# Reordering SyncE's DMA issues and two VectorE steps in one iteration of a gated cross-attention kernel

## The reference, cut to what matters

```python
n = layernorm(x)
q, k, v = n @ Wq + bq, ctx @ Wk + bk, ctx @ Wv + bv      # 16 heads of 16
e = einsum('nqhd,nkhd->nhqk', q, k);  e = where(mask == 0, min, e)
a = einsum('nhqk,nkhd->nqhd', softmax(e / sqrt(16)), v)
x = x + tanh(g_xattn) * (a @ Wo + bo)
x = x + tanh(g_ffn) * tanh(layernorm(x) @ W1 @ W2 @ W3 + b_ffn)
```

## Time and profile before

| | |
|---|---|
| median of 3 runs | 1143.55 us (1141.15 to 1146.37) |
| the profiled execution, its own time | 1153.29 us |
| its span, first to last instruction | 1151.5 us |
| mean granted TensorE clock | 0.978 |
| PE busy | 1041.1 us, 90% |
| DVE, ACT, POOL busy | 937.6 us (81%), 834.5 us (72%), 801.2 us (70%) |
| DMA moved | 158.87 MB, mean 138 GB/s; SP's queue 48.5% of 16 engines |

### The profile page before, as it was taken

How to read it: one execution, slowest core, us unless ns; L and a number is a source line. 1 busy time by engine, 2 the same in 40 slices (tenths; PEclk the granted TensorE clock), 3 DMA queues, 4 the chain that set the end, 5 groups by cost and what they waited for, 6 DMA issues and landing times.

```text
span 1151.5 us, 45278 instructions
## 1 busy us (share of the span) xinstructions
PE 1041.1 (90%) x18487; PEld 905.1 (79%) x18487; DVE 937.6 (81%) x1331; ACT 834.5 (72%) x1275; POOL 801.2 (70%) x1184
## 2 busy tenths in 40 slices
PE   5989989999999999999999989989999999999964
PEld 4767878887888888888778778878788788888854
DVE  4778788788888888888888788788887787888766
ACT  4466778677787777777787777777776786777742
POOL 5256677677777777777777777677776676777753
PEclk9899999999999999999999999999998999999998
DMA  5134455555555555555555455555545454554432
GB/s 154 41 95 128 130 141 152 139 142 153 145 155 139 154 152 145 148 154 155 139 154 143 140 150 144 144 145 144 161 133 138 139 144 137 140 159 122 115 114 90
DMA packets 260400, 158.87 MB, mean 138 GB/s; under 512 B 174945, under 2 KB 227170, under 8 KB 260194
## 3 DMA queue, kind: packets, MB, share of 16 engines
q1 hardware_dynamic: 260050, 155.72, 48.5%
q10 hardware_dynamic: 144, 0.26, 0.1%
HBM read 85.92 MB, written 68.94 MB: 134 GB/s over the span
## 4 chain that ended last, share of the span: by engine, by line
PE 34%; DMA 26%; SPq 23%; issue 11%; DVE 5%; POOL 1%; ACT 0%; DVEq 0%; POOLq 0%
DMA scratch_y<-yn 12%; PE ps_m L502 8%; PE ps_s L623 6%; SPq L299 6%; PE ps_s L602 6%; DMA q_aug<-scratch_m 5%; SPq L288 4%; DMA scratch_m<-max_T 4%; PE ps_m L564 4%; PE ps_m L495 4%; SPq L271 3%; PE ps_x L634 2%; PE ps_s L608 2%; SPq L258 2%; SPq L281 2%
## 5 line engine op out<-in xcount | busy, mean ns | idle before, releaser
L1006 DVE TENSOR_TENSOR probs<-ps_s,far_T 128x2048 f32<-128x2048 f32 x128 | 293.3, 2291 | 99.5 <-PE ps_s L623 93.2
L995 DVE TENSOR_REDUCE neg_max<-ps_s 128x16 f32<-128x2048 f32 x128 | 292.6, 2286 | 60.0 <-PE ps_s L608 59.8
L797 ACT ACTIVATE probs<-probs 128x2048 f32<-128x2048 f32 x128 | 244.6, 1911 | 6.7 <-DVE probs L1006 6.6
L623 PE MATMUL ps_s<-q_aug,k_aug 32*128 32x128 f32 x4096 | 155.4, 289 | 62.7 <-DMA q_aug<-scratch_m 59.1
L623 PEld LDWEIGHTS ps_s<-q_aug,k_aug 32*128 32x128 f32 x4096 | 130.3, 191 | 83.4 <-DMA q_aug<-scratch_m 69.1
L413 POOL TENSOR_TENSOR cT<-ctx_T,cT 128x512 fp32r<-128x512 f32 x62 | 79.2, 1277 | 151.6 <-ACT cT L747 151.6
L772 ACT ACTIVATE q_aug<-ps_m,q_bias,q_scale 128x256 f32<-128x256 f32 x256 | 123.4, 562 | 70.9 <-PE ps_m L495 63.3
L602 PE MATMUL ps_s<-k_aug,q_aug 32*128 32x128 f32 x4096 | 151.9, 284 | 14.4 <-DVE probs L1006 7.4
L602 PEld LDWEIGHTS ps_s<-k_aug,q_aug 32*128 32x128 f32 x4096 | 129.3, 187 | 35.1 <-issue 27.4
L634 PE MATMUL ps_x<-probs,v_ones 128*32 128x128 f32 x4096 | 139.2, 277 | 3.2 <-issue 2.4
L772 ACT ACTIVATE k_aug<-ps_m,k_bias,parity 128x256 f32<-128x256 f32 x256 | 123.5, 564 | 18.1 <-PE ps_m L495 18.1
(11 more groups left out here) (123 smaller groups left out, 1789.5 us busy)
## 6 DMA issues: line engine op xcount, KB each, us to landing
scratch_a<-a_den SPq DMA_DIRECT2D x64, 512.0 KB, 3.4
x_in<-in_x SPq DMA_DIRECT2D x64, 256.0 KB, 3.9
a_rows<-scratch_a SPq DMA_DIRECT2D x64, 256.0 KB
den_wide<-scratch_r SPq DMA_DIRECT2D x64, 256.0 KB
out<-y SPq DMA_DIRECT2D x64, 256.0 KB, 4.9
ctx_in<-in_ctx SPq DMA_DIRECT2D x252, 64.0 KB, 3.4
scratch_y<-yn SPq DMA_DIRECT2D x59, 256.0 KB, 4.7
y_blocks<-scratch_y SPq DMA_DIRECT2D x236, 64.0 KB, 2.1
```

The lines of the kernel that those rows point to most:

```text
L623: last = nc.tensor.matmul(ps_s[:, j, s, :], k_aug[p % 2][rows, n, s, :], q_aug[p % 2][rows, n, s, :], start=True, stop=True, tile_position ...
L797: nc.scalar.activation(tile, tile, ACT.Exp).then_inc(probs_ready, 1)
L995: nc.vector.tensor_reduce(neg_max[:, 0:H].rearrange("p (j c) -> p j c", j=G), ps_s[:], AX.X, ALU.max, negate=True).then_inc(max_ready, 1)
L1006: nc.vector.tensor_tensor(probs[i % 2][:].rearrange("p j s q -> p (j s) q"), ps_s[:].rearrange("p j s q -> p (j s) q"), far_T[:].unsqueeze ...
```

## The change

In SP's loop:

- `load_ctx(t+3)` moves from behind `store` to behind `load_x`;
- `read_max(2t)` moves ahead of `write_a(t-2)` and `load_x(t+4)`, so that only `read_den` stands between it and `write_max(2t)`;
- `write_y(t-4)` moves from the end of the iteration to ahead of `read_max(2t+1)`, and so ahead of `read_wide(t-2)` too.

In DVE's loop `turn_max(2t)` moves ahead of `add_residual` and `turn_ctx`, `turn_ctx` goes behind `add_residual`, and `turn_max(2t+1)` moves ahead of `reciprocals`. Nothing is added or removed.

```diff
@@ SP
                 if is_pair(t - 7):
                     store(t - 7)
-                if is_pair(t + 3):
-                    load_ctx(t + 3)
                 if is_pair(t - 5):
                     read_y(t - 5)
                 write_max(2 * t)
                 if is_pair(t - 2):
                     read_den(t - 2)
+                read_max(2 * t)
+                if is_pair(t - 2):
                     write_a(t - 2)
                 if is_pair(t + 4):
                     load_x(t + 4)
-                read_max(2 * t)
+                if is_pair(t + 3):
+                    load_ctx(t + 3)
                 write_max(2 * t + 1)
                 if is_pair(t - 2):
                     write_reciprocals(t - 2)
                     read_a(t - 2)
+                if is_pair(t - 4) and t - 4 <= END:
+                    write_y(t - 4)
                 read_max(2 * t + 1)
                 if is_pair(t - 2):
                     read_wide(t - 2)
-                if is_pair(t - 4) and t - 4 <= END:
-                    write_y(t - 4)
@@ DVE
                     maxima(2 * t)
-                if is_pair(t + 2):
-                    turn_ctx(t + 2)
                 turn_max(2 * t)
                 if is_pair(t - 4):
                     add_residual(t - 4)
+                if is_pair(t + 2):
+                    turn_ctx(t + 2)
@@ DVE
                     maxima(2 * t + 1)
+                turn_max(2 * t + 1)
                 if is_pair(t - 2):
                     reciprocals(t - 2)
-                turn_max(2 * t + 1)
```

## The result

| | before | after |
|---|---|---|
| median, 9 runs each | 1143.04 us (1136.36 to 1151.53) | 1148.67 us (1141.73 to 1150.54) |
| ratio after to before | | 1.0069, 95% interval 1.0037 to 1.0102 |
| the profiled execution | 1153.29 us | 1147.69 us |
| its span, mean granted clock | 1151.5 us, 0.978 | 1145.9 us, 0.990 |
| median in a later comparison, on another chip | 1157.74 us | 1148.28 us, ratio 0.9939 (0.9910 to 0.9967) |

The forecast was 1131 us, a gain of 1.1%. In the comparison that answers to it the change costs 0.7%; in a later one it wins 0.6%. The changed kernel's time hardly moves between the two, that of the kernel before moves by 15 us. Why is part of what follows.

What follows compares the result with a forecast made beforehand. PE works 90% of the span; at most 59 us of its waits for late maxima could be won. A POOL ring of 16.8 against 17.02 us left 12.5 us: 1143.55 - 12.5 = 1131 us, range 1102 to 1163.

Steps and rivals of the forecast that it cites:

- The maxima: PE's wait ahead of scores_T(2t): even maxima come up to 2.3 us earlier, 59 us to be had.
- the ring: Loop from read_wide through POOL's divide_a to yn, then SP's write_y and back to read_wide: 16.8 us, the period's floor.
- The moved transfers: SP's load_ctx, write_a and load_x ahead of the odd write_max: 0.5 to 1.5 us later, covered, cost nothing.
- The new wait and its ring: SP's write_y waits for yn ahead of read_wide, closing a loop through POOL: 10.80 + 1.70 + L.
- L: Time from issue of read_wide to the start of the divide_a it releases: taken as 4.3 us, bounds 4.22 and 5.50.
- The frame: Time scale of one undisturbed PE iteration, scores(2t) at 608.29, the next at 624.27; old write_y put at 15.9 us.
- The first rival: The ring is slower than the old loop, L 4.8 to 5.09: 1160 to 1176 us, chance 0.23.
- The sum: Whole loop: 17.02 - 16.8 = 0.22 us in 57 iterations, 12.5 us off the median 1143.55, giving 1131 us.
- SP's own chain: Rival: SP's steps from write_y on, 16.85 us, set the period; loop at 17.0, 1140 to 1146 us, chance 0.2.
- Ring order: DMA queue rule: transfers behind read_wide never slowed it, write_y ahead does; L would stay about where it was.

Runs made afterwards that it cites:

- max_only: The kernel before with only read_max(2t) moved ahead of write_a and load_x: 1121.21 us, ratio 0.968.
- write_y_only: The kernel before with only write_y moved ahead of read_max(2t+1) and read_wide: 1151.17 us, ratio 0.995.
- ctx_first: The changed kernel with load_ctx alone put back behind store: 1151.68 us, ratio 0.995 to the kernel before.
- dve_only: The kernel before with only the DVE swaps (turn_max and turn_ctx order): 1151.07 us, ratio 0.998.
- wide_first: The changed kernel with read_wide moved ahead of write_y in SP's order: 1184.59 us, ratio 1.028 to the kernel before.
- ring_shorter: The changed kernel with POOL's add_out_bias moved from between divide_a and yn to behind yn: 1100.50 us, ratio 0.953 to the kernel before.
- ring_longer: The changed kernel with one extra 128 x 512 POOL step between divide_a and yn: 1191.54 us, ratio 1.034 to the kernel before.

## Why the prediction was wrong

**The maxima.** Right in the total: 59.1 us of waits fell to 1.6, and the mean granted clock went from 0.978 to 0.990. Not right in the parts. The prediction gave 1.8 of the 2.3 us to the earlier `write_y` and 0.5 to `read_max(2t)`. Alone, the move of `read_max` took these waits to 6.2 us (max_only) and the earlier `write_y` to 53.3 (write_y_only). The part that closes the ring was not the part that won the maxima.

**The moved transfers.** Right in the cost, nothing. The delay was overrated: in the rows above, the odd `write_max` is issued at 622.65, 1.2 us after its maxima are turned (621.20 + 0.21, DVE's timeline), inside the 0.5 to 1.5 us foreseen. But that is one of the later ones. In 30 of the 56 iterations it leaves within 0.1 us, and the mean is 0.34 us. No wait of PE for it appeared, and ctx_first shows that `load_ctx` costs nothing where it now stands, as long as the ring sets the pace.

**The new wait and its ring.** Right in the mechanism, and shown by dose and response. POOL's chain was put at 10.80 us (10.75 measured), SP's part at 1.70 (1.65), the release of PE by xn as described (62.8 us of waits). The 10.80 hold two shifts that cancel: on average xn is 0.4 us shorter and the short steps ahead of it 0.4 us longer than in the kernel before (the last section). The frame's 15.9 us for the old `write_y` should be 16.4 (624.66 - 608.29); nothing was worked out from it.

**L, the failed size.** I took 4.3 us "near the low end, because a write of y leaves SBUF quickly". No row showed a write of y ahead of that read, and L measured 4.57 on average. That makes the ring 16.99 instead of 16.8 us, which is 57 x 0.19 = 11 us. The forecast missed by 17.7. The first rival had its turning point at 4.52, and this is where the kernel landed, only far closer to it than the 4.8 to 5.09 that I had priced.

**The base of the difference, the failed step.** The sum took 17.02 us as the old period, from an execution of 1153.3 us, set the ring of 16.8 against it, and then carried the difference of 12.5 us over to the median of 1143.55. That is allowed only if both kernels scale alike. A ring made of POOL steps and one landing does not shrink when the other kernel has a good run. At the median of 1143.04 the old period is 17.02 - (1151.5 - 1141.2) / 57 = 16.84 us, with 1141.2 the median less the 1.8 us that lie around the span. Against it my own ring of 16.8 promised 2 us, "no change", and the measured 16.99 gives 57 x 0.15 = 8.6 us more, where 5.6 were measured between the medians. This step cost the forecast 57 x 0.18 = 10 us, about as much as L did. Comparing the ring with the old kernel's median, not with its profiled execution, would have given no change as the forecast, and "slower" a larger chance.

**Outside the loop, a term put at nothing.** "The first iterations have no y, and the tail is untouched" was not so. `turn_max` of iteration 6 starts at 121.00 us instead of 126.20, and from iteration 62 to the end of the span it is 73.6 us instead of 72.4, so 4.0 us were won outside the 56 iterations. The second profiles say the same (120.54 against 126.08, and 73.8 against 72.3). Which part of the change brings the start forward stays open (dve_only alone starts that step at 123.36). With it the account closes: 11 + 10 - 4 = 17 of the 17.7 us missed, and 8.6 - 4.0 = 4.6 of the 5.6 us between the medians.

**SP's own chain.** Its 16.85 us was too long: in the changed kernel SP waits 96.4 us for yn in 59 iterations, so its chain takes 17.0 - 1.6 = 15.4 us, and 0.4 us of that is waiting for max_T (21.8 us in the 56 iterations). The write of y lands in 3.2 us (median) and not in 4.7, since the 256 KB of `read_wide` are no longer just ahead of it (wide_first, which puts them back, has 4.9), and issuing ctx took 2.5 us in the median, not the 3.65 of the earlier trace rows, which was one of the slow ones in the kernel before as well (median 2.8).

**Ring order.** The Trainium skill (DMA: Bandwidth & Descriptors, Queues, rings and completion order) says that each DMA engine consumes descriptors in ring order. From that I had worked out that L would stay near 5.1. What stands behind `read_wide` indeed hardly matters: with ctx behind it L is 4.68 in ctx_first, without 4.57. But a write of y 1.6 us ahead slows it less than `read_a` 2 us ahead did (5.17 on average in the first profile of the kernel before, 4.89 in the second). The rule does not tell these two apart, and the measured 4.57 decides. How far ahead `read_a` stands goes with L: within ring_shorter L is 5.25 on average in the 15 iterations where it is 2.2 to 2.7 us ahead, and 4.64 in the 15 where it is 3.2 us or more.

## What to carry to other kernels

When a step that waits for another engine is moved ahead of others in a queue, follow what stands behind it until the path comes back to the same wait: if it does, the sum of that ring is a floor for the period, and idle time on the engines in it is no cover. Then compare the floor with the old kernel's own range of times, not with the one execution that was profiled, since waits that vary are replaced by one that does not. And once a ring is named, look for a step in it that nobody inside needs: here moving one 1.2 us addition out of it turned a change worth about nothing into one of 4.7%.

## What the runs showed of the hardware

A short step of POOL takes longer while a certain step of DVE runs. In the rows of the changed kernel above, a step on 128 x 4 elements at 621.48 takes 0.76 us, where its neighbours take 0.20. DVE's timeline has, at that time,

```profile
621.56 0.63 DVE L958 TENSOR_TENSOR yT<-y_T,yT 128x512 fp32r<-128x512 f32 x1
```

and the end of the POOL step (622.24) is just behind the end of this one (622.19). In the changed kernel 63 of these short steps (without L371, which takes 1.04 us in nearly every case) take over 0.4 us, and 58 of them overlap this DVE step; another 20 overlap it and stay short. One iteration earlier it is another step, again beside L958:

```profile
604.90 0.56 POOL L379 TENSOR_TENSOR ln_t<-ln_t 128x4 f32<-128x4 f32 x1
```

```profile
604.78 0.63 DVE L958 TENSOR_TENSOR yT<-y_T,yT 128x512 fp32r<-128x512 f32 x1
```

It belongs to the ring's 10.75 us. In the kernel before the same DVE step falls on xn: in the earlier trace rows the two instructions of xn take 1.60 us where those of yn take 1.09, and DVE has

```profile
200.84 0.65 DVE L957 TENSOR_TENSOR yT<-y_T,yT 128x512 fp32r<-128x512 f32 x1
```

It also explains ring_longer, whose 1.00 us of extra work lengthened the chain by only 0.76. There the short steps meet the DVE step less often (18 of them over 0.4 us, instead of 58), and the seven of a turn take 2.21 us instead of 2.49. One of them, first in the changed kernel and then in ring_longer (busy us, mean ns, idle us before it):

```profile
L377 POOL TENSOR_SCALAR ln_t<-ln_t 128x4 f32<-128x4 f32 x69 | 31.5, 456 | 6.4
L378 POOL TENSOR_SCALAR ln_t<-ln_t 128x4 f32<-128x4 f32 x69 | 14.5, 210 | 6.4
```

That the overlap is the cause rests on these counts; no run moved the DVE step alone.

Behind the wait of 2.30 us in the earlier trace rows the granted clock was 0.68 on average for 5.3 us, between the levels of 1.2 and 2.4 GHz; the waits of at most 1.5 us for xn in the changed kernel, though there is one in nearly every iteration, left the mean at 0.99.
